# Two issues of row maxima moved from SyncE to ScalarE, and the last load of context moved two slots later, in a fused transformer block

## The chip, the cores and the metric

The kernel runs on one core of one Trainium2 chip. The metric is the time of one execution in microseconds on the device. Unless something else is said, times in the text are microseconds from the start of the profiled span.

## What is computed

One block of a diffusion transformer with self attention, cross attention and an MLP, for 32 sequences of 128 tokens with 128 channels, 16 heads of 8, and a context of 77 tokens. All tensors are float32.

```python
c_proj = silu(c) @ W_mod + b_mod
shift_a, scale_a, gate_a, shift_m, scale_m, gate_m = split(c_proj, 6)
q, k, v = split(modulate(ln(x), shift_a, scale_a) @ W_qkv + b_qkv, 3)
x = x + gate_a * (softmax(q k^T * scale) v @ W_proj + b_proj)
q_c = ln(x) @ W_qc + b_qc
k_c, v_c = split(ln(context) @ W_kvc + b_kvc, 2)
x = x + softmax(q_c k_c^T * scale) v_c @ W_cproj + b_cproj
h = gelu(modulate(ln(x), shift_m, scale_m) @ W_mlp1 + b_mlp1)
return x + gate_m * (h @ W_mlp2 + b_mlp2)
```

## The kernel before

**Tiling.** The 32 sequences are worked in 16 pairs (numbered 0 to 15). A pair goes through a pipeline of slots: in the slot of pair n, pair n + 2 is normalised ("far"), pair n + 1 gets its queries and keys ("ahead"), pair n has its self attention ("here"), pair n - 1 finishes it, and pairs n - 2 and n - 3 ("back2", "back3") have their cross attention. Each engine has a function `slot(s)` that writes down its own share of the slot in a fixed order; `h` is the pair "here", `a` "ahead", `f` "back2", `e` "back3". The first slots are -2 to 3, written out one by one, then a hardware loop runs over the slots 4 to 13, and 14 and 15 are written out again. The slots of pairs 1, 2 and 3 begin at 34.6, 51.3 and 68.9 us in the trace. "The first slot" of the title's change is that of pair 0, so the second, third and fourth are those of pairs 1, 2 and 3. `Pair.first(m)` is true for pairs below m where the number is a constant, so not in the loop.

**A slot in eight beats.** TensorE, VectorE and ScalarE go through beats t = 0 to 7. In beats 0 to 3 TensorE forms the scores of pair n in four units (`scores`, L1347), from which VectorE takes row maxima (`maxima`, L862). From beat 5 on it forms the scores again, transposed (`scores_t`, L1358), and ScalarE takes exponentials of them (`exps`, L1080), from which TensorE forms the sums with the values (`values`, L1369). The self attention's last unit and the next slot's first come together.

**Operand stacks.** Float32 accuracy in the scores is had from bf16 pieces: queries and keys are split into three bf16 pieces each by GpSimd (L606 to L620), and six products of pieces are stacked along the partitions of `qk_st`. The stack is built by six DMAs per pair from SyncE's queue (`stack`, L387): one in `SELF_ORDER[0]`, three in `SELF_ORDER[1]`, two in `SELF_ORDER[2]`. TensorE's first score unit of a pair waits for all six. `qkc_st` is the same for the cross attention.

**Rows of maxima.** The negated row maxima take part in the transposed scores as two more rows of the stack. VectorE's maxima (`mx`) are split into two bf16 pieces by GpSimd (`split_max`, L637 and L639), transposed by TensorE (`max_t`, L1459), copied out by ScalarE (`empty_max`, L1093, into `nmT`) and put into the stack by two small DMAs (`max_rows`, L436). This is done once for each sequence of the pair: b = 0 in beat 3, b = 1 in beat 5. TensorE waits for them before the transposed scores of unit 0 and of unit 2 (semaphores `m_in..`).

**Order of SyncE's queue.** SyncE issues all of these in the order of its `slot`: the cross stack of "back2" and rows of "back3", the first piece of the stack "ahead", the rows b = 0 of "here", three pieces, the rows b = 1, the last two pieces, the cross rows of "back2". In the slot of pair 1 the rows b = 0 come first, and `load_c(4)` stands behind the last two pieces. Each issue waits on its semaphore, and everything behind it waits with it.

**Loads.** The context comes in five loads (`load_c(0)` to `load_c(4)`, L412) of 2, 6, 8, 8 and 8 sequences; the last is of sequences 24 to 31, 308 KB. Loads 2 and 3 are issued behind the slot of pair 0. VectorE's part of the slot waits for them in `arrived`, in beat 4 of pair n's slot ahead of the statistics of pair n's context (L825):

```python
if t == 4 and h:
    arrived("c_in", h, {0: (0,), 1: (1,), 3: (2, 3, 4)})
    stats("ctx", h, ctx_of(h))
    aggregate("ctx", h)
```

so in the slot of pair 3 it waits for loads 2, 3 and 4 at once. Right behind it in the same beat come the cross maxima of "back2".

Of the kernel before, what the change touches and what calls it, by code (L numbers as in the profile page):

```python
# [24 lines left out]
B, T, C = 32, 128, 128  # L25
H, D = 16, 8
# [19 lines left out]
HALF = 64  # L46
KROWS = 62
# [145 lines left out]
def block_kernel(nc, x, cond, ctx, w_mod, b_mod, w_qkv, b_qkv, w_proj, b_proj, w_qc, b_qc, w_kvc, b_kvc,  # L193
# [5 lines left out]
    with es:  # L199
        def sb(name, shape, dt=f32):  # L200
            return es.enter_context(nc.sbuf_tensor(name, shape, dt))

        def pairbuf(name, shape, dt=f32):
            return [sb(f"{name}{i}", shape, dt) for i in range(2)]

        sems = {}
# [36 lines left out]
        qk_st = pairbuf("qk_st", [128, NM, 2, GT], bf16)  # L243
        qkc_st = pairbuf("qkc_st", [128, NM, 2, GT], bf16)
# [23 lines left out]
        nmT = sb("nmT", [2 * H, G, T], bf16)  # L268
        nmcT = sb("nmcT", [2 * H, G, T], bf16)
# [74 lines left out]
        def w(eng, name, value):  # L344
            eng.wait_ge(sems[name], value)

        def hold(eng, name, value):

            eng.wait_ge(sems[name], value)
            eng.sem_inc(sems[f"held_{eng.engine.name}"], 1)  # L350
# [31 lines left out]
        def stack(queue, dst, parts, name, chosen):  # L382


            for a, b in chosen:
                c = COMBOS.index((a, b))
                queue.dma_start(dst[c:128:ROWSTEP], parts[:].rearrange("c a p t -> c (a p) t")[:, a:b + 4:b + 3 - a]  # L387
                                ).then_inc(sems[name], 16)

        block = es.enter_context(nc.Block())  # L390


        @block.sync
        def _(sp):
# [15 lines left out]
            def load_c(n):  # L410
                lo, hi = PIECES[n:n + 2]
                sp.dma_start(ctx_sb[:, lo:hi], ctx[lo:hi].rearrange("b t c -> t b c")).then_inc(sems[f"c_in{n}"], 16)  # L412
# [18 lines left out]
                halves(3, b_kvc, 0, "bc_in")  # L431
            load_x(2)

            def max_rows(dst, b, src, name):
                for r in range(2):
                    sp.dma_start(dst[KROWS + r:128:HALF, :, 0, b * T:(b + 1) * T],  # L436
                                 src[r * H:(r + 1) * H, b]).then_inc(sems[name], 16)

            def slot(s):
                a, h, f, e = (s.pair(n) for n in ("ahead", "here", "back2", "back3"))  # L440
                if f:
                    if f.first(2):
                        w(sp, "zq_set", 4)
                        w(sp, "zk_set", 4)
                    hold(sp, "kc2_set", f.n + 1)
                    hold(sp, "qch_set", f.n + 1)
                    if not f.first(2):
                        w(sp, "stc_ps", 2 * NU * (f.n - 1))
                    stack(sp, qkc_st[f.par], qkcp, f"qkc_in{f.par}", CROSS_ORDER[0])
                if e:  # L450
                    w(sp, "nmcT_set", 2 * e.n + 2)
                    max_rows(qkc_st[e.par], 1, nmcT, f"mc_in{e.par}1")
                if f:
                    w(sp, "qc1_set", f.n + 1)
                    stack(sp, qkc_st[f.par], qkcp, f"qkc_in{f.par}", CROSS_ORDER[1])
                    w(sp, "qc2_set", f.n + 1)
                    stack(sp, qkc_st[f.par], qkcp, f"qkc_in{f.par}", CROSS_ORDER[2])
                if h and h.second():
                    w(sp, "nmT_set", 2 * h.n + 1)
                    max_rows(qk_st[h.par], 0, nmT, f"m_in{h.par}0")  # L460
                if a:
                    if a.first(2):
                        w(sp, "zq_set", a.n + 1)
                        w(sp, "zk_set", a.n + 1)
                    if a.first():
                        w(sp, "k0_set", 1)
                    hold(sp, "qkh_set", a.n + 1)
                    if not a.first(2):
                        w(sp, "st_ps", 2 * NU * (a.n - 1))
                    stack(sp, qk_st[a.par], qkp, f"qk_in{a.par}", SELF_ORDER[0])  # L470
                if h and not h.first(2):
                    w(sp, "nmT_set", 2 * h.n + 1)
                    max_rows(qk_st[h.par], 0, nmT, f"m_in{h.par}0")
                if a:
                    if a.first():
                        w(sp, "k0_set", 3)
                    w(sp, "qk1_set", a.n + 1)
                    stack(sp, qk_st[a.par], qkp, f"qk_in{a.par}", SELF_ORDER[1])
                if h and h.first():
                    w(sp, "nmT_set", 1)  # L480
                    max_rows(qk_st[h.par], 0, nmT, f"m_in{h.par}0")
                if a and a.second():
                    w(sp, "qk2_set", a.n + 1)
                    stack(sp, qk_st[a.par], qkp, f"qk_in{a.par}", SELF_ORDER[2])
                if h:
                    w(sp, "nmT_set", 2 * h.n + 2)
                    max_rows(qk_st[h.par], 1, nmT, f"m_in{h.par}1")
                if a:
                    if not a.first(2):
                        w(sp, "qk2_set", a.n + 1)  # L490
                        stack(sp, qk_st[a.par], qkp, f"qk_in{a.par}", SELF_ORDER[2])
                if h and h.second():
                    load_c(4)
                if s.left() == 1:
                    sp.dma_start(w1_sb[:], w_mlp1).then_inc(sems["w12_in"], 16)
                    sp.dma_start(w2_sb[:], w_mlp2.rearrange("(k f) c -> f k c", k=NF)).then_inc(sems["w12_in"], 16)
                    with nc.allow_non_contiguous_dma(reason="bias columns"):
                        sp.dma_start(b1_sb[:], b_mlp1.rearrange("(k c) -> c k", k=NF)).then_inc(sems["b1_in"], 16)
                if f:
                    w(sp, "nmcT_set", 2 * f.n + 1)  # L500
                    max_rows(qkc_st[f.par], 0, nmcT, f"mc_in{f.par}0")

            def between(s):
                if s == -1:
# [2 lines left out]
                if s == 0:  # L507
# [3 lines left out]
                    load_x(4)  # L511
                    load_c(3)
            slots(sp, slot, between)

            p13, p14, p15 = LAST[-3:]
# [2 lines left out]
            w(sp, "stc_ps", 2 * NU * (p14.n - 1))  # L518
            stack(sp, qkc_st[p14.par], qkcp, f"qkc_in{p14.par}", CROSS_ORDER[0])
            w(sp, "nmcT_set", 2 * p13.n + 2)  # L520
            max_rows(qkc_st[p13.par], 1, nmcT, f"mc_in{p13.par}1")
            w(sp, "qc1_set", p14.n + 1)
            stack(sp, qkc_st[p14.par], qkcp, f"qkc_in{p14.par}", CROSS_ORDER[1])
            w(sp, "qc2_set", p14.n + 1)
# [23 lines left out]
            for p in (p14, p15):  # L548
                for b in range(G):
                    w(sp, "nmcT_set", 2 * p.n + b + 1)  # L550
                    max_rows(qkc_st[p.par], b, nmcT, f"mc_in{p.par}{b}")

            def store(g, par):
                w(sp, "m_out_set", g + 1)
# [502 lines left out]
        def _(act):  # L1057
# [25 lines left out]
            def values(dst, keys, src):  # L1083

                return nc.scalar.activation(
                    bass_view(dst, keys), src.rearrange("t (x s d) -> t x s d", s=2, d=D), ACT.Copy)

            def empty_max(p, b, job, ready, dst, name, loaded):
                w(act, ready, 2 * p.n + b + 1)
                if not p.first():  # L1090
                    q = p.shift(-1)
                    w(act, f"{loaded}{q.par}{b}", 16 * 2 * (q.turn + 1))
                nc.scalar.activation(dst[:, b], ps_misc[BANK[job]][:].bitcast(bf16)[0:2 * H, 0:T],  # L1093
                                     ACT.Copy).then_inc(sems[name], 1)
# [74 lines left out]
            def slot(s):  # L1169
                a, h, d, f, e, z = (s.pair(n) for n in ("ahead", "here", "back1", "back2", "back3", "back4"))  # L1170
                for t in range(BEATS):
# [13 lines left out]
                        copy(cT[:], ps_misc[BANK["ctx_t"]][:, 0:GS], "ctxt_ps", d, "cT_set", "kvc_ps")  # L1185
                    if t == 5 and h:
                        empty_max(h, 1, "max_s1", "mts_ps", nmT, "nmT_set", "m_in")
                    if t == 6 and d:
                        w(act, "kvc_ps", d.n + 1)
                        src = ps_misc[BANK["kv_c"]]  # L1190
                        if d.first():
                            act.wait_ge(sems["zvc_set"], 1)
                            act.wait_ge(sems["bc_in"], 16 * 4)
                        else:
                            w(act, "kcr_set", d.n)
                        nc.scalar.activation(kcx[:], src[:, 0:GS], ACT.Identity, bias=bdh[:, 3:4])
                        if not d.first(2):
                            w(act, "pvc_ps", NU * (d.n - 1))
                        values(vc_m[d.par], S, src[0:S, GS:GS + G * C]).then_inc(sems["kvc0_set"], 1)
# [42 lines left out]
                if a and a.first():  # L1242
# [3 lines left out]
                    stack(act, qk_st[0], qkp, "qk_in0", SELF_ORDER[2])  # L1246
                    biased(a.shift(1))
            slots(act, slot)

            def cross_exps(p, units):  # L1250
# [9 lines left out]
            p12, p13, p14, p15 = LAST[-4:]  # L1260
# [510 lines left out]
```

## Time and profile before

| | us |
|---|---|
| median of 3 runs | 377.98 |
| the three runs | 373.79, 377.98, 378.31 |
| the profiled execution | 376.56 |
| its span, first to last instruction | 374.5 |
| mean granted TensorE clock | 0.986 of full |
| busy: TensorE, VectorE, ScalarE, GpSimd | 339.9, 263.8, 269.8, 210.0 |

PE is TensorE's matmul, PEld its weight load, DVE VectorE, ACT ScalarE, POOL GpSimd, SP SyncE; SPq and ACTq are DMA issues on SyncE's and ScalarE's queue, and the time of such a line is that of the issue, not of the transfer. In a line of the timeline the first number is the start, the second the time until the last of the merged instructions ends, xN how many there are, and in square brackets stands how long the engine was idle before it and what released it.

### The profile page before, as it was taken

The numbers are of one execution on the slowest core, as the hardware profiler recorded it, in microseconds if no ns is written. First come the engines' busy times: TensorE is split into PE (matmuls) and PEld (weight loads), VectorE is DVE, ScalarE is ACT, GpSimd is POOL, SyncE is SP. The second block draws the span as 40 slices with busy tenths as digits, with TensorE's granted clock in tenths as the row PEclk, the third lists the DMA queues.
The fourth block names the chain that finished last, engine by engine and source line by source line (L and its number), as shares of the span: only waits on it lengthen the run. The fifth ranks groups of instructions, "written<-read, shape, count | busy, mean of one in ns | idle before, by whom it ended". The sixth has DMA issues, their size and how long they took to land. (4 is left out here: it accounts for less than half of the span.)

```text
span 374.5 us, 16029 instructions
## 1 busy us (share of the span) xinstructions
PE 339.9 (91%) x5888; PEld 231.6 (62%) x5888; DVE 263.8 (70%) x671; ACT 269.8 (72%) x526; POOL 210.0 (56%) x479
## 2 busy tenths in 40 slices
PE   4677877899899999999999999999798999999996
PEld 3455545577676767777677777767665445554444
DVE  6956658698878889887888979888766754443401
ACT  2336465878888887888879888888776756776673
POOL 6862666777767787777877777777455220112100
PEclk9998889999999999999999999999999999999999
DMA  5744552444344444434344344444324200102001
GB/s 131 155 104 129 140 148 59 95 112 104 86 103 106 100 103 97 101 86 111 93 111 112 74 100 114 100 110 96 89 72 98 68 4 3 30 28 56 28 28 56
DMA packets 65788, 33.13 MB, mean 88 GB/s; under 512 B 8471, under 2 KB 65495, under 8 KB 65751
## 3 DMA queue, kind: packets, MB, share of 16 engines
q1 hardware_dynamic: 63847, 32.36, 35.6%
q10 hardware_dynamic: 1904, 0.27, 0.6%
q8 instruction: 24, 0.39, 0.5%
q14 instruction: 13, 0.11, 0.1%
HBM read 4.83 MB, written 2.10 MB: 18 GB/s over the span
## 5 line engine op out<-in xcount | busy, mean ns | idle before, releaser
L862 DVE TENSOR_REDUCE mx<-wide 128x8 f32<-128x1024 f32 x64 | 78.2, 1221 | 26.4 <-PE wide L1347 26.1
L1080 ACT ACTIVATE p_c<-wide 128x1024 f32<-128x1024 f32 x64 | 65.5, 1023 | 21.5 <-PE wide L1358 20.5
L1080 ACT ACTIVATE p_s<-wide 128x1024 f32<-128x1024 f32 x64 | 65.7, 1026 | 12.5 <-PE wide L1358 12.2
L862 DVE TENSOR_REDUCE mxc<-wide 128x8 f32<-128x616 f32 x64 | 50.7, 792 | 4.4 <-PE wide L1347 4.0
L1369 PE MATMUL ps_o<-p_s,v_m 128*32 128x128 f32 x1024 | 42.4, 284 | 0.2
L1369 PE MATMUL ps_o<-p_c,vc_m 128*32 128x128 f32 x1024 | 41.3, 279 | 0.3 <-ACT p_c L1080 0.3
L1347 PE MATMUL wide<-qk_st 62*128 62x128 bf16 x512 | 26.6, 226 | 11.7 <-DMA qk_st<-qkp 6.6
L1347 PEld LDWEIGHTS wide<-qk_st 62*128 62x128 bf16 x512 | 15.2, 97 | 27.9 <-DVE mx L862 13.0
L1410 PE MATMUL wide<-m_nT,w_sb 128*128 128x512 f32 x64 | 30.1, 600 | 0.2 <-DVE mxc L862 0.2
L1369 PEld LDWEIGHTS ps_o<-p_s,v_m 128*32 128x32 f32 x1024 | 25.0, 111 | 7.5 <-issue 1.9
L1369 PEld LDWEIGHTS ps_o<-p_c,vc_m 128*32 128x32 f32 x1024 | 24.1, 109 | 7.0 <-issue 0.5
L1358 PE MATMUL wide<-qk_st 64*128 64x128 bf16 x512 | 25.9, 221 | 1.8 <-ACT p_s L1080 1.4
L1358 PE MATMUL wide<-qkc_st 64*128 64x128 bf16 x512 | 25.1, 216 | 1.3 <-ACT p_c L1080 0.8
L643 POOL TENSOR_TENSOR m_ve<-m_mv,eps_sb 128x4 f32<-128x4 f32 x8 | 1.6, 199 | 42.4 <-DVE m_mv L898 42.4
L601 POOL TENSOR_TENSOR x_rstd<-x_ve,mhalf 128x2 f32<-128x2 f32 x32 | 22.5, 702 | 3.5 <-POOL x_ve L596 1.9
L879 DVE TENSOR_TENSOR xs<-xs,ps_misc 128x256 f32 (+1 forms) x32 | 13.5, 420 | 15.3 <-PE ps_misc L1515 8.0
L1125 ACT ACTIVATE qk_st<-wide,b_sb 128x512 f32<-128x512 f32 x32 | 20.6, 694 | 1.8 <-PE wide L1410 1.5
L1418 PE MATMUL ps_o<-qk_st,w_sb 128*128 128x512 f32 x48 | 21.9, 595 | 0.0
L637 POOL CAST nm<-mx 128x16 bf16<-128x16 f32 x32 | 6.3, 196 | 27.7 <-DVE mx L862 14.6
L841 DVE TENSOR_SCALAR x_n<-xs,x_mv,x_rstd 128x128 f32 (+1 forms) x64 | 19.9, 354 | 2.3 <-POOL x_rstd L601 2.3
L1347 PE MATMUL wide<-qkc_st 62*128 62x77 bf16 x512 | 20.1, 201 | 1.1 <-DVE mx L862 0.5
L919 DVE TENSOR_TENSOR m_out<-xs,ps_misc 128x512 f32<-128x512 f32 x7 | 4.8, 687 | 22.9 <-PE ps_misc L1427 22.8
(182 smaller groups left out, 822.9 us busy)
## 6 DMA issues: line engine op xcount, KB each, us to landing
qk_st<-qkp SPq DMA_DIRECT2D x94, 128.0 KB, 2.5
qkc_st<-qkcp SPq DMA_DIRECT2D x90, 128.0 KB, 2.5
out<-m_out SPq DMA_DIRECT2D x7, 256.0 KB, 2.3
xs<-x SPq DMA_DIRECT2D x3, 512.0 KB, 5.1
qk_st<-nmT SPq DMA_DIRECT2D x64, 4.0 KB
qkc_st<-nmcT SPq DMA_DIRECT2D x64, 4.0 KB
ctx_sb<-ctx SPq DMA_DIRECT2D x3, 308.0 KB
w_sb<-L_xcond_W_mlp SPq DMA_DIRECT2D x2, 256.0 KB, 3.0
```

Of the source, the lines that this page charges most:

```text
L601: nc.gpsimd.tensor_tensor(L["rstd"][:], L["ve"][:], mhalf[0:L["rows"], 0:G], ALU.pow).then_inc(sems[f"{kind}_rstd_set"], 1)
L637: nc.gpsimd.tensor_copy(nmt[:, b, 0], mxt[:, b]).then_inc(sems[high], 1)
L841: nc.vector.tensor_scalar(L["xn"][:, b], src(b), L["mv"][:, b, 0:1], L["rstd"][:, b:b + 1], ALU.subtract, ALU.mult).then_inc(sems[f"{kind} ...
L862: nc.vector.reduce_max(mxt[:, b].rearrange("q (x r) -> q r x", r=2)[:, r], src, AX.X, negate=True).then_inc(sems[done], 1)
L879: nc.vector.tensor_tensor(xs[:, batches(p)], xs[:, batches(p)], ps_misc[BANK[job]][:, 0:GT].rearrange("t (b c) -> t b c", b=G), ALU.add).t ...
L1080: nc.scalar.activation(dst[u % 2][:].rearrange("k x q -> k (x q)"), ps_st[:].rearrange("k s x -> k (s x)"), ACT.Exp, scale=SCALE).then_inc ...
L1125: nc.scalar.activation(hT[par][:, k], h_bank(g, k), ACT.Gelu_apprx_tanh, bias=b1_sb[:, k:k + 1]).then_inc(sems["m_hT_set"], 1)
L1347: last = mm(ps_max[:, s_, j * T:j * T + keys], st[p.par][lo:lo + KROWS, m, 0, b * T:(b + 1) * T], st[p.par][lo:lo + KROWS, m, 1, b * T:b * ...
L1358: last = mm(ps_st[:, s_, j * T:(j + 1) * T], st[p.par][lo:lo + HALF, m, 1, b * T:(b + 1) * T], st[p.par][lo:lo + HALF, m, 0, b * T:(b + 1) ...
L1369: last = mm(ps_o[32 * j:32 * j + 32, at:at + T], vt[p.par][:, b, 4 * j + 2 * r + s_], probs[u % 2][:, 4 * s_ + j], start=(s_ == 0), stop=( ...
L1410: mm(h_bank(g, k), w1_sb[:, k * 128:(k + 1) * 128], m_nT[par][:], start=True, stop=True).then_inc(sems["m_h_ps"], 1)
L1418: last = mm(y_bank(g)[:, :], w2_sb[:, k], hT[par][:, k], start=(k == 0), stop=(k == NF - 1))
```

## The change

The helper `max_rows` moves out of SyncE's block and takes the queue as an argument. For pairs 1 and 2 the rows b = 1 are issued by ScalarE, right behind its copy of them in beat 5, after a wait for that copy; SyncE leaves them out in these two slots. `load_c(4)` moves from the end of pair 1's slot to pair 3's slot, behind the rows b = 0 and ahead of the three pieces of the stack. Nothing else changes: VectorE's waits stay as they are.

```diff
+        def max_rows(queue, dst, b, src, name):
+
+            for r in range(2):
+                queue.dma_start(dst[KROWS + r:128:HALF, :, 0, b * T:(b + 1) * T],
+                                src[r * H:(r + 1) * H, b]).then_inc(sems[name], 16)
+
+        def rows_by_act(h):
+
+            return h.first(3) and not h.first()
...
                 if h and not h.first(2):
                     w(sp, "nmT_set", 2 * h.n + 1)
-                    max_rows(qk_st[h.par], 0, nmT, f"m_in{h.par}0")
+                    max_rows(sp, qk_st[h.par], 0, nmT, f"m_in{h.par}0")
+                if h and h.first(4) and not h.first(3):
+                    load_c(4)
...
-                if h:
+                if h and not rows_by_act(h):
                     w(sp, "nmT_set", 2 * h.n + 2)
-                    max_rows(qk_st[h.par], 1, nmT, f"m_in{h.par}1")
+                    max_rows(sp, qk_st[h.par], 1, nmT, f"m_in{h.par}1")
                 if a:
                     if not a.first(2):
                         w(sp, "qk2_set", a.n + 1)
                         stack(sp, qk_st[a.par], qkp, f"qk_in{a.par}", SELF_ORDER[2])
-                if h and h.second():
-                    load_c(4)
...
                     if t == 5 and h:
                         empty_max(h, 1, "max_s1", "mts_ps", nmT, "nmT_set", "m_in")
+                        if rows_by_act(h):
+                            w(act, "nmT_set", 2 * h.n + 2)
+                            max_rows(act, qk_st[h.par], 1, nmT, f"m_in{h.par}1")
```

## Rows read from the trace of the kernel before

**Rows 1.** The page, busy time by engine: us, share of the span, instructions.
```profile
PE 339.9 (91%) x5888; PEld 231.6 (62%) x5888; DVE 263.8 (70%) x671; ACT 269.8 (72%) x526; POOL 210.0 (56%) x479
```

**Rows 2.** Busy time in stretches (from:to, length, engines, clock, DMA share, GB/s): pairs 2 to 4.
```profile
51.30:68.86 17.56, 13.86 (x230) 9.02 (x230) 12.51 (x29) 9.48 (x20) 11.27 (x27) 0.90 0.39 92
68.86:84.44 15.58, 15.08 (x332) 11.21 (x333) 12.67 (x28) 12.66 (x25) 11.61 (x26) 1.00 0.45 106
84.44:100.70 16.26, 15.72 (x353) 11.76 (x352) 13.80 (x33) 13.82 (x28) 11.97 (x28) 1.00 0.44 103
```

**Rows 3.** Timeline of TensorE, 20 to 70 us.
```profile
51.32 0.40 PE L1347 MATMUL wide<-qk_st 62*128 62x128 bf16 x8 [1.64 <-DMA qk_st<-qkp]
...
56.87 0.23 PE L1459 MATMUL ps_misc<-ident,nm 128*32 128x128 bf16 x1
...
65.55 0.60 PE L1436 MATMUL ps_misc<-ident,x_n 128*128 128x128 f32 x2 [0.59 <-DVE x_n L841]
...
68.86 0.40 PE L1347 MATMUL wide<-qk_st 62*128 62x128 bf16 x8 [0.92 <-DMA qk_st<-qkp]
```

**Rows 4.** Busy time in short stretches, columns as in rows 2.
```profile
51.30:53.30 2.00, 1.45 (x40) 1.07 (x40) 1.22 (x1) 1.30 (x3) 1.68 (x5) 1.00 0.71 161
53.30:56.40 3.10, 3.10 (x26) 1.77 (x20) 1.22 (x1) 1.02 (x3) 1.59 (x5) 0.50 0.59 150
40.00:43.00 3.00, 1.47 (x17) 1.17 (x17) 2.76 (x8) 0.96 (x3) 2.08 (x5) 1.00 0.38 85
44.00:46.00 2.00, 2.00 (x36) 1.28 (x28) 1.31 (x6) 1.02 (x1) 0.67 (x2) 0.50 0.54 125
58.00:61.00 3.00, 1.80 (x25) 1.36 (x25) 2.75 (x9) 0.96 (x3) 1.87 (x5) 1.00 0.20 46
```

**Rows 5.** Timeline of SyncE's DMA issues.
```profile
45.36 1.16 SPq L436 DMA_DIRECT2D qk_st<-nmT  x2
46.56 1.27 SPq L387 DMA_DIRECT2D qk_st<-qkp  x2
47.87 0.53 SPq L412 DMA_DIRECT2D ctx_sb<-ctx  x1
...
63.97 1.14 SPq L436 DMA_DIRECT2D qk_st<-nmT  x2
...
75.18 1.15 SPq L436 DMA_DIRECT2D qk_st<-nmT  x2
77.89 1.93 SPq L387 DMA_DIRECT2D qk_st<-qkp  x3
```

**Rows 6.** Timeline of GpSimd.
```profile
43.45 1.15 POOL L608 TENSOR_TENSOR qkp<-qkr,qkp 128x512 bf16<-128x512 f32 x1
...
52.94 0.70 POOL L601 TENSOR_TENSOR x_rstd<-x_ve,mhalf 128x2 f32<-128x2 f32 x1
54.90 0.20 POOL L637 CAST nm<-mx 128x16 bf16<-128x16 f32 x1 [1.26 <-issue]
```

**Rows 7.** Issues of line 387, 45 to 49 us: from issue to landing.
```profile
DMA to landing us min/median/max: 2.5/2.6/4.0
```

**Rows 8.** The same, 65 to 67 us (pair 3's last two pieces).
```profile
DMA to landing us min/median/max: 2.5/2.5/2.5
```

**Rows 9.** Issues of line 387 on ScalarE's queue, 12 to 20 us: ns min/median/max.
```profile
L387 ACTq DMA_DIRECT2D qk_st<-qkp x2: 666/682/697, 15.3 to 16.0; - x2
```

**Rows 10.** Timeline of ScalarE: first exponentials of pairs 1 and 2.
```profile
44.95 1.02 ACT L1080 ACTIVATE p_s<-wide 128x1024 f32<-128x1024 f32 x1 [1.47 <-PE wide L1358]
...
62.50 1.02 ACT L1080 ACTIVATE p_s<-wide 128x1024 f32<-128x1024 f32 x1 [1.03 <-PE wide L1358]
```

**Rows 11.** Timeline of VectorE, pair 3's slot.
```profile
76.57 0.47 DVE L825 BATCH_NORM_STATS2 ctx_stats<-ctx_sb 77x6 f32<-77x128 f32 x2
```

**Rows 12.** Issues of line 408 (loads of x, 512 KB), 32 to 35 us.
```profile
DMA to landing us min/median/max: 4.0/5.3/6.6
```

**Rows 13.** Timeline of TensorE's weight loads, pair 3's slot.
```profile
78.34 0.18 PEld L1347 LDWEIGHTS wide<-qkc_st 62*128 62x128 bf16 x8 [0.20 <-DVE mxc L862]
```

More of the change, by code:

```diff
@@ L432, in _ @@
             load_x(2)
[L434 to L437, printed above, removed]
             def slot(s):
@@ L451, in slot @@
                     w(sp, "nmcT_set", 2 * e.n + 2)
-                    max_rows(qkc_st[e.par], 1, nmcT, f"mc_in{e.par}1")
+                    max_rows(sp, qkc_st[e.par], 1, nmcT, f"mc_in{e.par}1")
                 if f:
@@ L472, in slot @@
                     w(sp, "nmT_set", 2 * h.n + 1)
-                    max_rows(qk_st[h.par], 0, nmT, f"m_in{h.par}0")
+                    max_rows(sp, qk_st[h.par], 0, nmT, f"m_in{h.par}0")
+                if h and h.first(4) and not h.first(3):
+                    load_c(4)
                 if a:
@@ L480, in slot @@
                     w(sp, "nmT_set", 1)
-                    max_rows(qk_st[h.par], 0, nmT, f"m_in{h.par}0")
+                    max_rows(sp, qk_st[h.par], 0, nmT, f"m_in{h.par}0")
                 if a and a.second():
@@ L500, in slot @@
                     w(sp, "nmcT_set", 2 * f.n + 1)
-                    max_rows(qkc_st[f.par], 0, nmcT, f"mc_in{f.par}0")
+                    max_rows(sp, qkc_st[f.par], 0, nmcT, f"mc_in{f.par}0")
             def between(s):
@@ L520, in _ @@
             w(sp, "nmcT_set", 2 * p13.n + 2)
-            max_rows(qkc_st[p13.par], 1, nmcT, f"mc_in{p13.par}1")
+            max_rows(sp, qkc_st[p13.par], 1, nmcT, f"mc_in{p13.par}1")
             w(sp, "qc1_set", p14.n + 1)
@@ L550, in _ @@
                     w(sp, "nmcT_set", 2 * p.n + b + 1)
-                    max_rows(qkc_st[p.par], b, nmcT, f"mc_in{p.par}{b}")
+                    max_rows(sp, qkc_st[p.par], b, nmcT, f"mc_in{p.par}{b}")
             def store(g, par):
```

## The prediction

> **What bounds the kernel now.** I read the page first: TensorE is busy for 339.9 of a span of 374.5 us [rows 1]. A share over the whole span does not say what one slot is worth, so I cut the trace into slots by the first score matmul of each pair. The slot of pair 2 has PE busy for 13.86 of 17.56 us at a granted clock of 0.90; the slots of pair 3 (15.08 of 15.58) and of pair 4 (15.72 of 16.26) run at 1.00 and are nearly full [rows 2]. So TensorE bounds the kernel from pair 3 on, and a shift of an earlier slot goes through to the end: nothing in the full slots can take up time or give it back. Whatever this change does, it does it between 43 and 85 us.
>
> The order of PE's work in time says what the early slots lack. Its first score matmul of a pair waits for the stack of operand pieces: 1.64 us ahead of pair 2 at 51.32 and 0.92 us ahead of pair 3 at 68.86 [rows 3]. Both waits lie behind an issue of row maxima that the change takes from SyncE. The granted clock of short stretches is the third view: 0.50 (1.2 of 2.4 GHz) for 3.1 us from 53.3, behind the first of these gaps and a thin stretch (PE busy 1.45 of 2.0 us). The 3 us from 40 to 43, with PE busy for 1.47, have a stretch at 0.50 behind them too [rows 4].
>
> **The change, part by part.** *Maxima of pair 1 off SyncE's queue.* SyncE issues the two rows at 45.36 for 1.16 us, then the last two pieces of pair 2's stack from 46.56 to 47.83 [rows 5]. GpSimd has these pieces ready at 44.6 [rows 6], so without the rows they go about 1.2 us earlier. *The load of context out of the same place.* It follows at 47.87 [rows 5], and the last piece, issued just before it, took 4.0 us to land [rows 7]; in the next slot, with no load behind it, the same pair of pieces took 2.5 [rows 8]. That is 1.5 us from the load's company. Together the stack would land at about 46.0 + 2.5 = 48.5 us. PE has its own work until 49.7 (51.32 less its wait), so the whole gap of 1.64 us closes, and no more than that: the gain is 1.6. Bounds: 1.16 (issue time alone) and 1.64.
>
> *The clock behind the gap.* With PE busy straight through, I expect the stretch at 0.50 to go. It holds 3.1 us [rows 4], all of it with PE busy, so at the full clock the same work takes half: 1.55 us. Bounds 0 and 1.55; I take 1.55 since the gap is the emptiest place ahead of the fall. Then something else is late: PE would reach the transpose of pair 2's maxima at 56.87 - 1.64 - 1.55 = 53.7 [rows 3], while GpSimd comes to their split only after its power operation ends at 53.64, and the split is a cast like the one at 54.90 (0.20) with a subtraction of about that length after it [rows 6]: some 0.5 us with the gap between them, so it is ready at 54.15. I take 0.4 off.
>
> *Maxima of pair 2.* The issue at 63.97 (1.14 us) [rows 5] stands ahead of pair 3's last two pieces, and PE waits 0.92 us for them [rows 3]. With 1.14 us gone from the queue the gap closes: gain 0.9, the bound being the gap itself.
>
> *What ScalarE pays.* Two issues in each slot. One of SyncE's takes 0.58 us (half of 1.16), one of ScalarE's own took 0.68 [rows 9], so 1.2 to 1.4 us for two, with a wait on its own copy. Behind the copy ScalarE now stands idle for 1.47 us in pair 1's slot and 1.03 us in pair 2's [rows 10]. In the first it costs nothing. In the second the exponentials start 0.2 to 0.4 us late, and who waits for them is PE's next transposed scores. PE idles 0.59 us at 65.55 for VectorE's normalised x, which does not depend on ScalarE here [rows 3]; that cover takes the delay. I take 0; with that cover gone it costs 0.3. The rows themselves, landing from ScalarE's queue, come earlier than before and nobody waits for them. The Trainium skill (DMA: Bandwidth & Descriptors, section Issuing engines are not separate DMA queues) says that transfers issued from several engines share the same 16 engines and only the issue time is saved, usually a small one. Taken alone it would allow 1.16 us in place of 1.6 at the first gap, and it is silent on the load. The trace has the issue time at a place where TensorE waits for it, so it counts here.
>
> *The load in pair 3's slot.* This is the cost. SyncE now issues it after pair 3's first rows, whose issue starts at 75.18 and lasts 1.15, so at 76.37 [rows 5]. VectorE's statistics of pair 3's context begin at 76.57 [rows 11], and in the code they wait for pieces 2, 3 and 4 of the context together: piece 4 too, though pair 3 uses nothing of it. Today all of them landed long before. After the change VectorE waits for a load that was issued 0.2 us earlier. For its latency I have two sides: 2.5 us for 128 KB [rows 8] and 4.0 us for the faster of two 512 KB loads of x [rows 12]. Between them by size, 308 KB is 2.5 + 180/384 x 1.5 = 3.2 us. It lands at 79.6, and VectorE stands for 3.0 us (2.3 to 3.8). Queued behind it are the slot's first cross maxima, and behind these PE's next cross scores: their weight load at 78.34 is released by just these maxima, after 0.20 us of idling [rows 13]. TensorE runs its instructions in order and these scores stand ahead of the transposed scores for ScalarE, so PE stops from 78.4 on and ScalarE behind it. The cost is the whole 3.0 us. SyncE loses nothing: the load's issue takes 0.53, to 76.9, and its next pieces wait for GpSimd until 77.89 [rows 5].
>
> *The clock behind that stop.* PE would be idle for 3.0 us on end, emptier than either stretch ahead of a fall in [rows 4]. I expect one more fall to 0.50 of about 3.1 us in a stage where PE is full: 1.5 us. Bounds 0 and 1.55.
>
> **The sum.** Gains: 1.6 + 1.55 - 0.4 + 0.9 = 3.7 us. Costs: 3.0 + 1.5 = 4.5. The difference is 0.8 us longer. The profiled execution took 376.56 us (span 374.5 and 2.1 around it), which gives 377.4. The median of the runs before is 377.98 and they go from 373.79 to 378.31, so the profiled one is 1.4 under the median and in the middle of the spread; I leave the sum at 377.4.
>
> **The rivals.** *The clock does not fall after the stop* (chance 0.17): costs 3.0 against gains 3.7, 375.9. For it: the slot is dense before and after, and between 58 and 61 us PE is busy for 1.80 of 3.0 us and the clock holds [rows 4]. Against: two falls behind stretches less empty than this.
>
> *The load is hidden* (0.08): it lands by the time VectorE comes, because the slots' order has moved or SyncE gets to it earlier than I read. Then only gains are left: 372.9. Against it stands that the load's issue hangs on the same copy of maxima as before, 0.2 us ahead of its reader.
>
> *Slower: only issue time is gained, and the stop costs in full* (0.20). The place is VectorE's wait in pair 3's slot, the price 3.0 + 1.5, and it decides as soon as the early gains are under that: 1.16 + 0.9 = 2.1 us, with the slow clock staying where it is (it falls at other places in these slots as well, so the gap need not be its cause). 376.56 + 4.5 - 2.1 = 379.0. With the longest latency (3.8) it is 379.8. The skill's rule on shared engines (same page and section) would go this way; against it is the row of 2.5 us where no load follows.
>
> *The change does not do what it says* (0.05): the stack of pair 2 lands late for another reason, such as GpSimd's pieces, and the load's move costs alone: 376.56 + 4.5 - 0.9 = 380.2. The pieces being ready at 44.6, a microsecond before SyncE is free, speaks against it.
>
> The forecast itself, gains and costs nearly cancelling, has 0.50.
>
> **The numbers.** Predicted 377.4 us. The range takes in the first rival and the slower one with their unknowns, a microsecond of spread on top, and leaves out the hidden load and the end beyond 380.3: 373.2 to 380.3. 2% is 7.5 us and about what a measurement of this kernel can tell from no change. No case reaches that: the fastest gives -3.7, the slowest +3.7. Faster by over 2%: 0.03; within 2%: 0.93; slower by over 2%: 0.04, for a clock that falls again and again.
>
> **What would show it.** Right: SyncE issues pair 2's last pieces right behind the three before them; the score matmul of pair 2 follows the query projection with no wait for the stack, and so does that of pair 3; two issues on ScalarE behind the copies of the second maxima; a wait of VectorE's context statistics in pair 3's slot of 2.3 to 3.8 us for the context load, with PE idle in its wake; the granted clock at 1.00 behind pair 2's start and at 0.50 behind that stop. Wrong: no wait of VectorE there, which makes it the hidden load; the last piece of pair 2 still landing in 4 us, which makes it issue time only; or ScalarE's exponentials late in pair 2's slot and PE waiting for them.

## The result, and the profile after

The changed kernel takes 379.3 us in the median (376.32 to 382.15, 22 runs), the kernel before 376.61 (372.79 to 379.68, 22 runs, the three known before among them). The ratio is 1.0089, 95% interval 1.006 to 1.0118: slower by 0.9%, inside the 2% that was called no change, clear of noise, and on the side that the predicted 377.4, a little under the known median of 377.98, did not say. The ratio is that of the means without the slow runs, those more than 1.5% above the fastest of their kernel (four of before, two of after), and so a little larger than that of the medians (1.0071). The measured time lies in the range of 373.2 to 380.3. The profiled execution of after has a span of 377.6 us and a granted clock of 0.994.

First the two places where time was to be won. TensorE's timeline of after, answering [rows 3]:

```profile
46.54 0.40 PE L1366 MATMUL wide<-qk_st 64*128 64x128 bf16 x8 [1.30 <-ACT p_s L1085]
...
48.99 0.70 PE L1463 MATMUL ps_misc<-x1T,wdh 128*128 128x256 f32 x2
49.62 0.40 PE L1355 MATMUL wide<-qk_st 62*128 62x128 bf16 x8
...
54.26 0.22 PE L1467 MATMUL ps_misc<-ident,nm 128*32 128x128 bf16 x1 [0.50 <-POOL nm L644]
...
60.92 0.40 PE L1366 MATMUL wide<-qk_st 64*128 64x128 bf16 x8 [0.58 <-ACT p_s L1085]
...
64.72 0.40 PE L1355 MATMUL wide<-qk_st 62*128 62x128 bf16 x8
```

Both waits for the stack are gone: pair 2's first scores follow the query projection at 49.62 (before 51.32), pair 3's start at 64.72 (before 68.86). The transpose of pair 2's maxima waits 0.50 us for GpSimd, for which the prediction took 0.4 off. The 1.30 at 46.54 and the 0.58 at 60.92 are new: TensorE waits there for exponentials that stand behind ScalarE's issues. SyncE's and ScalarE's issues, answering [rows 5] and [rows 10]:

```profile
41.18 5.92 SPq L387 DMA_DIRECT2D qk_st<-qkp  x6
...
71.49 1.15 SPq L393 DMA_DIRECT2D qk_st<-nmT  x2
72.68 0.42 SPq L422 DMA_DIRECT2D ctx_sb<-ctx  x1
74.00 1.93 SPq L387 DMA_DIRECT2D qk_st<-qkp  x3
```

```profile
43.78 1.57 ACTq L393 DMA_DIRECT2D qk_st<-nmT  x2
45.46 1.02 ACT L1085 ACTIVATE p_s<-wide 128x1024 f32<-128x1024 f32 x1 [1.71 <-issue]
...
58.47 1.27 ACTq L393 DMA_DIRECT2D qk_st<-nmT  x2
59.84 1.02 ACT L1085 ACTIVATE p_s<-wide 128x1024 f32<-128x1024 f32 x1 [1.40 <-PE wide L1366]
```

The six pieces of pair 2 go out without a gap, the last ends at 47.10, and it lands 2.5 us after its issue; the load is issued at 72.68, right behind pair 3's rows. Then the place of the loss, VectorE and TensorE in pair 3's slot, answering [rows 11] and [rows 13]:

```profile
71.56 1.22 DVE L867 TENSOR_REDUCE mx<-wide 128x8 f32<-128x1024 f32 x1
76.89 0.48 DVE L830 BATCH_NORM_STATS2 ctx_stats<-ctx_sb 77x6 f32<-77x128 f32 x2 [4.12 <-DMA ctx_sb<-ctx]
```

```profile
74.09 0.43 PE L1523 MATMUL ps_misc<-wg,oT 128*32 128x128 f32 x8
78.50 0.31 PE L1355 MATMUL wide<-qkc_st 62*128 62x77 bf16 x8 [3.98 <-DVE mxc L867]
```

VectorE stands for 4.12 us for the context load and TensorE for 3.98 us behind it. The clock follows (stretches as in [rows 4]; the seventh number is the granted clock):

```profile
50.00:52.00 2.00, 1.45 (x46) 0.97 (x44) 1.39 (x2) 2.00 (x5) 1.07 (x2) 1.00 0.20 41
52.00:54.00 2.00, 1.76 (x27) 0.97 (x16) 1.23 (x2) 1.31 (x4) 1.78 (x5) 1.00 0.80 192
76.00:78.00 2.00, 0.00 (x0) 0.00 (x0) 0.96 (x5) 0.00 (x0) 0.00 (x0) 1.00 0.67 153
80.00:82.00 2.00, 2.00 (x36) 1.34 (x33) 1.29 (x6) 1.32 (x5) 1.55 (x6) 0.50 0.04 8
```

It stays at 1.00 where it fell before (from 53.3), and falls to 0.50 (1.2 of 2.4 GHz) behind the stop, from 79.1 to 82.8. The two whole slots, from their first score matmul, against 17.56 and 15.58 us in [rows 2]:

```profile
49.62:64.72 15.10, 12.21 (x230) 8.10 (x230) 11.94 (x26) 9.52 (x21) 11.45 (x26) 1.00 0.44 106
64.72:85.79 21.07, 16.34 (x332) 12.14 (x333) 13.32 (x34) 13.69 (x27) 12.20 (x29) 0.92 0.39 94
```

So pair 3's slot is 5.49 us longer: TensorE stands idle 4.2 us more in it (21.07 less 16.34 busy, before 15.58 less 15.08), and its busy time is 1.3 us longer, which is the slow clock. The table follows all profiled kernels by one matmul that every slot has, the projection of queries and keys (L1580 before, L1588 after): its start in the slots of pairs 1 to 4 and 14, the span, and what is left from the last of these to the end.

| kernel | 1 | 2 | 3 | 4 | 14 | span | rest |
|---|---|---|---|---|---|---|---|
| before | 37.59 | 54.40 | 71.72 | 87.62 | 249.18 | 374.5 | 125.3 |
| before, again | 38.25 | 55.72 | 73.26 | 90.29 | 251.61 | 377.5 | 125.9 |
| after | 37.83 | 52.33 | 67.83 | 88.81 | 250.28 | 377.6 | 127.3 |
| after, again | 38.66 | 53.13 | 68.63 | 91.02 | 252.78 | 379.4 | 126.6 |
| wait late (e1) | 38.16 | 52.67 | 68.17 | 84.16 | 245.52 | 374.2 | 128.7 |
| rows only (e2) | 38.27 | 52.90 | 68.54 | 86.74 | 247.71 | 374.1 | 126.4 |
| load only (e3) | 37.50 | 54.50 | 72.70 | 93.81 | 255.19 | 381.6 | 126.4 |
| load in pair 2 (e4) | 38.43 | 53.10 | 68.75 | 84.65 | 245.69 | 371.9 | 126.2 |
| the same again (e9) | 37.59 | 52.04 | 67.53 | 83.58 | 245.40 | 371.2 | 125.8 |
| rows behind (e5) | 38.08 | 55.80 | 74.24 | 90.11 | 251.60 | 377.2 | 125.6 |
| small piece (e6) | 38.24 | 52.71 | 68.20 | 87.54 | 249.58 | 375.3 | 125.7 |
| load later (e7) | 38.12 | 52.59 | 68.08 | 93.15 | 255.16 | 381.7 | 126.5 |
| pair 14 too (e8) | 38.74 | 53.23 | 68.71 | 84.94 | 246.57 | 372.9 | 126.3 |

After against before: 4.1 us won between the first column and the third (0.24 behind, then 3.89 ahead), 5.1 lost from there to the fourth. From pair 4 on the two run side by side (1.19 and 1.10 us behind). The rest of the 3.1 us between the spans, 2.0, lies behind pair 14. In the second pair of profiles (both "again") it is 5.0 us won, 5.4 lost, and 0.7 behind pair 14.

What the early gain is made of, the stretch from the first column to the third, before and then after (the second number is its length, the third TensorE's busy time, the seventh the clock):

```profile
37.59:71.72 34.13, 26.57 (x434) 17.40 (x435) 22.64 (x55) 19.30 (x41) 22.64 (x50) 0.90 0.45 110
```

```profile
37.83:67.83 30.00, 23.36 (x438) 15.67 (x434) 22.61 (x55) 19.28 (x41) 22.05 (x49) 1.00 0.44 108
```

3.2 us of the 4.1 are busy time, so the clock, and only 0.9 are idle time, though the two gaps that closed had 2.56 us between them.

### The profile page after: what moved, and what is told of

It is laid out like the page before. It is cut to its first block and busy times, and to the rows that moved or that the text cites. A ratio compares the mean times of both kernels' runs of the same rounds, so it can differ in the third digit from the quotient of the medians.

```text
span 377.6 us, 16029 instructions
## 1 busy us (share of the span) xinstructions
PE 338.4 (90%) x5888; PEld 230.9 (61%) x5888; DVE 264.0 (70%) x671; ACT 270.3 (72%) x526; POOL 210.3 (56%) x479
## 5 line engine op out<-in xcount | busy, mean ns | idle before, releaser
L1355 PEld LDWEIGHTS wide<-qkc_st 62*128 62x128 bf16 x512 | 11.9, 97 | 18.6 <-DVE mxc L867 8.5
L642 POOL CAST nmc<-mxc 128x16 bf16<-128x16 f32 x32 | 6.3, 197 | 27.9 <-issue 18.9
```

The source lines that it names most:

```text
L642: nc.gpsimd.tensor_copy(nmt[:, b, 0], mxt[:, b]).then_inc(sems[high], 1)
L1355: last = mm(ps_max[:, s_, j * T:j * T + keys], st[p.par][lo:lo + KROWS, m, 0, b * T:(b + 1) * T], st[p.par][lo:lo + KROWS, m, 1, b * T:b * ...
```

## The experiments

**e1, the wait where the data is needed.** Is VectorE's wait the loss?

```diff
                     if t == 4 and h:
-                        arrived("c_in", h, {0: (0,), 1: (1,), 3: (2, 3, 4)})
+                        arrived("c_in", h, {0: (0,), 1: (1,), 3: (2, 3)})
...
                     if t == 7 and h:
+                        arrived("c_in", h, {3: (4,)})
                         normalise("ctx", h, ctx_of(h), "ctxt_ps")
```

> The changed kernel with one edit: VectorE waits for context load 4 in beat 7 of pair 3's slot, no longer in beat 4; the load stays where the change put it. Theory A (VectorE's wait of 4.1 us and the 3 us of slow clock behind it are the whole loss): the wait and the slow stretch are gone, pair 3's slot takes 15.6 us again in place of 21.1, the early gain of 4 us stays, so 3.5 to 4.5 us under the kernel before. Theory B (a good part of the loss sits in SyncE's queue in the last slots, where the changed trace loses 2 us against the one before): only 1.5 to 2.5 us under the kernel before, with the extra waits at 262 to 302 us still in the trace. Theory C (the traffic of the load beside the stack's pieces in pair 3's slot costs by itself): TensorE waits for the stack of pair 4 ahead of its slot, gain 3 or less.

Measured: 375.61 us against 377.45 before, ratio 0.9973 (0.9939 to 1.0007). That is 1.0 us by the ratio and 1.8 by the medians, not theory A's 3.5 to 4.5. But between the third and the fourth column stand 15.99 us again in place of 20.98, and in the slot of pair 14 this kernel is 3.7 us ahead of the profile of before. The wait and the clock behind it are the 5 us, with the load's transfer just where the change put it, so theory C falls. By the ratios (1.0089 and 0.9973) the edit is worth 4.4 us of the changed kernel's time. The profiled execution gives most of it back in the rest, 128.7 us, where TensorE waits 1.62 us for pair 15's stack and 1.27 us for its cross queries and the clock falls once more (0.78 and 0.80 in the stretches of 4 us from 296 to 304): theory B is not out yet.

**e2, the rows alone.**

```diff
-                if h and h.first(4) and not h.first(3):
-                    load_c(4)
...
                         stack(sp, qk_st[a.par], qkp, f"qk_in{a.par}", SELF_ORDER[2])
+                if h and h.second():
+                    load_c(4)
```

> The first half of the change alone: rows b = 1 of pairs 1 and 2 on ScalarE's queue, load 4 back at the end of pair 1's slot. Theory A (issue time and the load's company both hold up pair 2's stack): the last piece is issued 1.2 us earlier but still takes up to 4 us to land, so TensorE's wait ahead of pair 2 shrinks from 1.64 to 0.5 us, the one ahead of pair 3 goes, 2 us under the kernel before, up to 3.5 if the slow clock goes too. Rival (issue time alone was in the way): the wait ahead of pair 2 is gone, 3.5 to 4 us under.

375.01 us, ratio 0.9937 (0.9901 to 0.9974): 2.4 us faster. TensorE's wait ahead of pair 2 is gone with the load behind the pieces, and the last piece lands in 2.5 us. The trace is the rival's: the load's company had cost nothing. The time is not, 2.4 us in place of 3.5 to 4, nearer to theory A's 2. This execution lost 2.28 us in pair 3's slot, waiting for a cross piece that landed late.

**e3, the load alone.**

```diff
         def rows_by_act(h):
-            return h.first(3) and not h.first()
+            return False
```

> The second half of the change alone: load 4 moved to pair 3's slot with VectorE's wait left as it is, all rows on SyncE's queue. Theory A: the last piece of pair 2's stack lands in 2.5 us, the wait ahead of pair 2 shrinks by about 1.5 us, the one ahead of pair 3 stays at 0.9, and pair 3's slot loses 5.5 us: 2.5 to 4 us slower than the kernel before. Rival (the load's place behind pair 2's stack cost nothing): the wait ahead of pair 2 stays, 5 to 6 us slower.

383.23 us, ratio 1.0146 (1.0082 to 1.021): 5.5 us slower by the ratio, the rival's number. Landing times of the stack's pieces issued between 46 and 49 us, first of e3 (no load behind them), then of e2 (load behind them):

```profile
DMA to landing us min/median/max: 2.5/3.3/4.1
```

```profile
DMA to landing us min/median/max: 2.5/2.6/2.9
```

The late landing belongs to SyncE's order with the rows ahead of the pieces, not to the load. TensorE's timeline of e3 has the wait for the stack and the one behind VectorE:

```profile
51.34 0.40 PE L1355 MATMUL wide<-qk_st 62*128 62x128 bf16 x8 [1.74 <-DMA qk_st<-qkp]
...
83.53 0.32 PE L1355 MATMUL wide<-qkc_st 62*128 62x77 bf16 x8 [4.13 <-DVE mxc L867]
```

**e4 and e9, the load in pair 2's slot**, behind the cross stack, with the rows on ScalarE. Measured twice.

```diff
                     stack(sp, qkc_st[f.par], qkcp, f"qkc_in{f.par}", CROSS_ORDER[2])
+                if h and h.first(3) and not h.first(2):
+                    load_c(4)
```

> The changed kernel with load 4 issued in pair 2's slot, right behind the cross stack of pair 0 and some 15 us ahead of VectorE's wait, which stays in beat 4 of pair 3. Theory A: no wait of VectorE, no traffic beside a stack that TensorE waits for, so the same as with the late wait: 3.5 to 4.5 us under the kernel before. Theory B (the queue's last slots cost 2 us whatever the load does): 1.5 to 2.5 us under.

> The kernel with load 4 in pair 2's slot once more, unchanged, beside the one that also moves pair 14's rows: 2 to 3.5 us under the kernel before, as in its first measurement (ratio 0.9945).

374.05 us, ratio 0.9945 (0.9909 to 0.9981), and 374.12 us, ratio 0.9954 (0.9914 to 0.9995). Faster than both kernels, and the shortest spans of the study, 371.9 and 371.2. In e4's profile the load is issued at 55.02, 18.6 us ahead of its reader, while SyncE waits for GpSimd anyway. By the medians and by the ratios it is 5 us under the changed kernel: the same rows on ScalarE, the same number of issues, only no wait. Against the kernel before it is 2.1 and 1.7 us by the ratios (3.4 and 2.7 by the medians), less than theory A's 3.5 to 4.5 and inside theory B's 1.5 to 2.5, though up to pair 14 both profiles are 3.5 and 3.8 us ahead.

**b0 and a0, both kernels profiled again.**

> The kernel before, profiled once more, unchanged. Theory D (the last piece of pair 2's stack lands in 4 us because of its place in SyncE's queue behind two small issues): again 4.0 us, TensorE waits 1.6 us ahead of pair 2. Rival (a chance event of one execution): 2.5 us and a wait near 0. Theory B (the queue's last slots are slower in the changed kernels only): from the last full slot to the end 125 us as before, TensorE waits about 1.0 us for pair 15's stack. Rival (that stretch varies from one execution to the next): 126 us or more, 1.5 us or more.

> The changed kernel, profiled once more, unchanged. VectorE's wait for context load 4 is again 4.1 us and the granted clock is 0.50 for 3 us behind it (theory A), the last piece of pair 2's stack lands in 2.5 us again (theory D). Theory B: 127 us or more from the last full slot to the end; rival: anything from 125 to 129.

379.63 and 381.45 us. The last piece of pair 2's stack took 4.2 us to land in the kernel before and 2.5 in the changed one, where VectorE waited 4.38 us for the load and the granted clock was 0.50 for 6.8 us behind it, twice as long as expected. So the late landing is tied to its place: 4.0, 4.2 and 4.1 us in all three profiles with the rows ahead of this piece (before, again, e3), 2.4 to 2.6 in the other ten. The rest is 125.9 and 126.6 us; TensorE's wait for pair 15's stack, the first that I had seen longer in after, is 1.62 us here in the kernel before:

```profile
266.02 0.40 PE L1347 MATMUL wide<-qk_st 62*128 62x128 bf16 x8 [1.62 <-DMA qk_st<-qkp]
```

**e5, the rows behind the pieces, on SyncE.** Does it take ScalarE's queue?

```diff
-                if h:
+                if h and not (h.first(3) and not h.first()):
                     w(sp, "nmT_set", 2 * h.n + 2)
                     max_rows(qk_st[h.par], 1, nmT, f"m_in{h.par}1")
                 if a:
                     if not a.first(2):
                         w(sp, "qk2_set", a.n + 1)
                         stack(sp, qk_st[a.par], qkp, f"qk_in{a.par}", SELF_ORDER[2])
+                if h and h.first(3) and not h.first():
+                    w(sp, "nmT_set", 2 * h.n + 2)
+                    max_rows(qk_st[h.par], 1, nmT, f"m_in{h.par}1")
```

> The kernel before with one edit: for pairs 1 and 2 SyncE itself issues the rows b = 1, but behind the last two pieces of the stack instead of ahead of them; load 4 stays. Theory D: the last piece lands in 2.5 us, the wait ahead of pair 2 goes, but the rows come 1.3 us later and TensorE waits for them ahead of the third unit of transposed scores, 1 to 2 us in each slot: the time is the same as before or up to 1.5 us less, so ScalarE's queue is needed for the gain. Rival (anything on the queue right behind the pieces delays their landing): 4 us again, and slower than before by 1 to 2 us.

380.19 us, ratio 1.0077 (1.0044 to 1.011), slower by 2.8 us. The pieces land in 2.8 us at most, but TensorE now waits for the rows:

```profile
49.60 0.61 PE L1361 MATMUL wide<-qk_st 64*128 64x128 bf16 x8 [1.55 <-DMA qk_st<-nmT]
...
68.79 0.40 PE L1361 MATMUL wide<-qk_st 64*128 64x128 bf16 x8 [2.23 <-DMA qk_st<-nmT]
```

In both slots SyncE has two things that TensorE needs at once. I had expected the same time or a little less: the price of the later rows was above the gain, 2.23 us in pair 2's slot against the 0.9 that was there to win. It takes a second queue.

**e6, a smaller load 4.**

```diff
-                lo, hi = PIECES[n:n + 2]
+                lo, hi = [0, G, B // 4, B // 2, B - 4, B][n:n + 2]
```

> The changed kernel with context load 4 of 4 sequences (154 KB) in place of 8 (308 KB); load 3, issued behind pair 0's slot, takes the other 4. VectorE's wait stays in beat 4. Theory A with a latency that grows with size and with traffic beside it: the wait falls from 4.1 to about 3 us, 1 us under the changed kernel. Rival (the latency is fixed, or set by the pieces of the stack that are issued 1.3 us behind the load): 3.8 us or more, no gain over the changed kernel.

377.75 us, ratio 1.0018 (0.999 to 1.0047). VectorE waits 3.49 us, 0.6 less than in after, and from the load's issue to its reader's start it is 3.3 us against 4.2 for half the bytes, so size is the smaller part of the latency. By the ratios the kernel is 2.7 us under the changed one, more than the shorter wait gives; between the third and the fourth column this execution has 1.65 us less. This execution too lost 2.08 us to a late cross piece, hidden in the same stop of TensorE.

**e7, the load later still**, behind the three pieces of pair 4's stack.

```diff
                     stack(sp, qk_st[a.par], qkp, f"qk_in{a.par}", SELF_ORDER[1])
+                if h and h.first(4) and not h.first(3):
+                    load_c(4)
```

> The changed kernel with load 4 issued still later in pair 3's slot, behind the three pieces of the stack instead of ahead of them; VectorE's wait stays. Theory A (the cost is the time from the load's issue to its landing, and TensorE stands for all of it): the issue moves from 72.7 to about 75.9, so VectorE waits 7.2 us in place of 4.1, TensorE stands 7 us, and the kernel is 3 us slower than the changed one, 6 us slower than the one before. Rival (behind the pieces the load has the DMA engines for itself and lands 1 to 1.5 us sooner after its issue): 1.5 to 2 us slower than the changed one.

383.18 us, ratio 1.0169 (1.0087 to 1.0252). VectorE in pair 3's slot:

```profile
80.11 0.48 DVE L830 BATCH_NORM_STATS2 ctx_stats<-ctx_sb 77x6 f32<-77x128 f32 x2 [7.09 <-DMA ctx_sb<-ctx]
```

Issued at 76.22, which is 3.5 us later than in after, it makes the wait 3.0 us longer and pair 3's slot 4.1 us longer (25.07 against 20.98). By the ratios the kernel is 3 us slower than the changed one, as theory A had it. The reader starts 3.9 us after the load's issue, 0.3 less than in after, not the 1 to 1.5 of the rival. Here too a cross piece landed late, and TensorE stood 2.03 us for it ahead of the 4.91 behind VectorE. The time is of four runs alone.

**e8, pair 14's rows on ScalarE too**, on top of e4.

```diff
-            return h.first(3) and not h.first()
+            return h.first(3) and not h.first() or isinstance(h.n, int) and h.n == NPAIR - 2
```

> The kernel with load 4 in pair 2's slot, and ScalarE issuing the rows b = 1 of pair 14 too, where TensorE waits 1.0 to 1.9 us in every trace for pair 15's stack. If SyncE's issue time is what is late there as in pairs 1 and 2: the wait shrinks by 1.2 us, and the kernel is 1 us under the one with load 4 in pair 2's slot, 3.5 to 5 us under the kernel before. Rival (ScalarE is full in that slot, 8.0 of 10 us, and its exponentials are late by the issue time): no gain.

374.31 us, ratio 0.9932 (0.9898 to 0.9967); beside it e9 had 374.12. TensorE's wait for pair 15's stack is gone, and something else waits in its place:

```profile
255.97 0.40 PE L1366 MATMUL wide<-qk_st 64*128 64x128 bf16 x8 [0.67 <-ACT p_s L1085]
...
261.84 0.40 PE L1355 MATMUL wide<-qk_st 62*128 62x128 bf16 x8 [0.18 <-DVE mx L867]
...
267.84 0.32 PE L1355 MATMUL wide<-qkc_st 62*128 62x77 bf16 x8 [0.80 <-DMA qkc_st<-qkcp]
```

0.67 us for ScalarE's exponentials and 0.80 us for the cross stack take 1.5 us, about what was won at the stack (1.58 in e9). The two kernels can't be told apart, so the microsecond that was expected did not come.

## Why the prediction was wrong

Two steps failed. The stop behind the moved load was sized at 3.0 us and measured 4.1 to 4.4. And the end of the kernel was put at nothing, where the times of many runs leave 1.6 to 2.2 us. The point forecast was also set under the known median. In detail:

**The early gain was right in size, in part by luck.** Predicted 3.7 us, measured 4.1 and 5.0 by the table. Both gaps closed, the clock held, GpSimd's split became the next thing late. But the sum had 2.1 us of waits and 1.55 of clock, and the first pair of profiles has 0.9 and 3.2. The stretch at 0.50 that the sum took as 3.1 us lasts 3.4, to 56.7, and the one from 43.1 to 46.5 is gone too, which the sum did not have. In its place TensorE waits the 1.30 us at 46.54; e2 and e4 have that slow stretch still and no such wait, and come to the second column in the same time (14.63 and 14.67 us, after 14.50).

**One of its reasons was wrong.** The step said: "The load of context out of the same place", with 1.5 us from "the load's company". It named the right row (4.0 against 2.5 us) and the wrong cause. With the load gone and the rows kept (e3) the piece still took 4.1 us; with the load kept and the rows gone (e2) it took 2.5. Everything won came from the rows. Rows ahead are not enough, since pair 3's last pieces had them too and took 2.5 [rows 8]. Why a piece behind two small issues lands 1.5 us late at this place, and the like of it elsewhere (a cross piece in e2, e6 and e7), stays open. The Trainium skill (DMA: Bandwidth & Descriptors, section Issuing engines are not separate DMA queues) allows a second issuing engine only the sequencer's issue time, usually a small one. The trace agrees that SyncE's issue time is saved, 1.16 us a slot, and has one thing more: the landing shortened too, which comes of the order and not of the second queue (2.6 us in e5, all on SyncE). The two together were worth 2.4 us of the whole kernel (e2).

**ScalarE's price was not quite nothing.** For pair 1's slot the prediction said "In the first it costs nothing", from an idle time of 1.47 us that lies in the slow stretch of that one execution. Where the clock is at 1.00 there, in the kernel before profiled again, TensorE waits 0.32 us for the same exponentials, with the issues on ScalarE 1.30:

```profile
45.98 0.40 PE L1358 MATMUL wide<-qk_st 64*128 64x128 bf16 x8 [0.32 <-ACT p_s L1080]
```

Little of it is left at the end of the slot: that execution of before waits 0.29 us for VectorE's x and 0.26 for the rows behind this place, after waits for neither. For pair 2's slot the prediction said "I take 0; with that cover gone it costs 0.3": the exponentials made TensorE wait 0.58 us at 60.92. The cover was there as named: TensorE's wait for VectorE's x at 65.55 is gone from the profile after, so next to nothing of it is left over.

**The load's latency is the term that was mis-sized.** The stop was taken as 3.0 us (2.3 to 3.8) from a line between 128 KB and 512 KB. It measured 4.12 and 4.38 us (4.28 in e3), above my upper bound, which I took from the faster of two loads in [rows 12] (4.0) when the other had 6.6. Halving the bytes took 0.9 us off the time from issue to reader and issuing behind the three pieces 0.3 (e6, e7); the most of it stayed in both. The clock was sized about right in after, 1.3 us against 1.5, so the stop is what makes pair 3's slot cost 5.5 in place of 4.5. In after again the slow stretch lasted 6.8 us, beyond the bound of 1.55 us of cost (between the third and the fourth column TensorE is busy for 18.14 us, and 15.86 in before again). That the wait is the cause and not the traffic is shown by e1.

**The end of the kernel I had not looked at.** I wrote that a shift "goes through to the end". It does up to pair 14, but the rest takes 125.3 to 125.9 us in three profiles with the rows on SyncE and the load where it was (before, again, e5) and 125.7 to 128.7 in the others. The 2.0 us of the first pair of profiles are three waits: pair 15's stack 1.66 us against 1.02, the rows of pair 14 0.44 us, which before does not wait for, and pair 15's cross queries 0.90 us, of which SyncE issues one piece for 1.52 us where 0.60 is usual (the first line is from the chain of work that ended last):

```profile
297.92 1.52 SPq L539
```

```profile
301.68 0.32 PE L1355 MATMUL wide<-qkc_st 62*128 62x77 bf16 x8 [0.90 <-DMA qkc_st<-qkcp]
```

e1, e3, e7 and e8 wait there too (1.27, 0.61, 1.12, 1.12 us), the other eight profiles, after again and both of before among them, do not. It comes and goes with the execution of one and the same kernel; whether it comes more often once SyncE's stream has changed was not settled. The medians of many runs put after 2.7 us above before (by the ratio 3.4), the slots up to pair 14 account for 1.1 in the first pair of profiles and 1.2 in the second. That the other 1.6 to 2.2 us lie in the rest is what subtraction leaves, argued and not shown.

**The balance.** Gains and costs were close to each other, as forecast; a sum of +0.8 that needs two terms of 4 us to cancel hangs on the bounds of each, and of the misses the latency and the end went one way, the early gain (0.4 us more than predicted) the other. By the table the stretch that the prediction worked out came to 0.95 and 0.32 us longer in the two pairs of profiles, where the sum had 0.8. The range held the time. The point forecast was put on the profiled execution, 1.4 us below the known median, and so came out as a shade faster than that median where its own sum said slower.

## What to carry to other kernels

A load that is moved has a reader, and what counts is where the reader *waits*, not where the data is first used: here the wait stood nine pairs ahead of the use, and the move put issue and wait 0.1 us apart. Moving either one of them (e1, e4) turned a loss of 0.9% into a gain of 0.5% (e4) or one of 0.3% whose interval touches none (e1). Two issues of half a microsecond each are worth a second queue when the transfer behind them is the one that the busy engine waits for, and e5 shows how to ask: reorder on the same queue and see whether the wait only changes its name. A late landing seen beside another transfer is no proof that the one made the other late; take each away alone.

## What the runs showed of the hardware

- A 128 KB transfer of a stack landed 2.5 us after its issue in the median of every profile and within 3.2 in nine of ten. The last piece of pair 2 took 4.0 to 4.2 in three profiles out of three with two 4 KB issues ahead of it, with or without a 308 KB load behind it, and with the DMA engines busy for a share of 0.12 from 49 to 50 us and for nothing from 50 to 51 in e3, before it had landed at 51.2. Every profile has later ones as well: 3.5 to 5.2 us for six pieces between 13 and 17 us, and 3.6 to 4.5 for a cross piece between 280 and 291 us.
- A load of 308 KB took 3.9 to 4.5 us from its issue to its reader's start (after, after again, e3, e7), one of 154 KB 3.3 (e6).
- TensorE's granted clock was at 0.50 around the end of each stop of about 4 us or more, from between 1.1 us before that end and 0.7 behind it: for 3.4 us in after and e3, for 6.8 in after again and e7. Shorter stops were followed by both: in e6 0.50 for 3.4 us around a stop of 2.08, in e5 for 6.8 around one of 1.55 and for 3.4 behind one of 2.23, in before for 3.4 behind one of 1.64 and a thin stretch, in before again for 6.8 around one of 2.10, but in e2 1.00 all around one of 2.28. Behind pair 2's start it was 1.00 in after, where the gap of 1.64 us had gone.
- ScalarE's issue of two 4 KB transfers took 1.14 to 1.57 us, SyncE's 1.04 to 1.19.
